# Windowed attention, MLP and linear attention in one kernel: separate orders for even and odd steps, and the second final product in another PSUM bank

## What is computed

```python
# x: (8, 128, 32, 32) float32; C=128, windows of 8x8 = 64 tokens, 8 heads of 16
win = x in windows                                  # (B*16, 64, 128)
q, k, v = split(layernorm(win) @ in_w.T + in_b)     # per head
o = softmax(q @ k.T / 4) @ v
win = win + o @ out_w.T + out_b
y = win back in rows, channels last
y = y + silu(layernorm(y) @ fc1_w.T + fc1_b) @ fc2_w.T + fc2_b     # hidden 256
# second layer, linear attention over the N=1024 tokens of an image, E=64
q, k, v = wq @ y + bq, wk @ y + bk, wv @ y + bv
out = wo @ ((q.T @ k) / N @ v.T).T + bo + y
```

## Time and profile before

| | us |
|---|---|
| median of 3 runs | 371.51 (369.45 to 372.06) |
| the profiled execution | 368.75 |
| its span, first to last instruction | 367.0 |
| outside the span | 1.75 |
| PE, DVE, ACT, POOL busy in the span | 325.3, 278.4, 243.9, 165.0 |
| mean granted TensorE clock | 0.956 of full |

### The profile page before, as it was taken

The page is one execution under the profiler, slowest core; times in us unless marked ns, Lnnn a source line. Parts: engine busy times, 40 slices in busy tenths (PEclk is TensorE's granted clock), DMA queues, the critical chain, the costliest instruction groups (busy, mean ns, idle before and its releaser), DMA issues. The chain is left out here.

```text
span 367.0 us, 9985 instructions
## 1 busy us (share of the span) xinstructions
PE 325.3 (89%) x3424; PEld 275.4 (75%) x3424; DVE 278.4 (76%) x850; ACT 243.9 (66%) x449; POOL 165.0 (45%) x177
## 2 busy tenths in 40 slices
PE   6958798989899899989898999989898999977875
PEld 6847686869787887869686887869686977856563
DVE  5565588968699887978799687978799878694652
ACT  5447476866869586757869386757869496853360
POOL 5504264645527262636437162636437352622420
PEclk9999699989999999989999899989999999998995
DMA  5230203030322123130403123130403122210011
GB/s 132 65 94 17 65 23 96 18 103 0 82 92 60 55 57 114 29 86 4 139 29 76 39 56 115 27 87 4 139 29 73 41 67 79 50 38 2 0 60 57
DMA packets 31859, 21.99 MB, mean 60 GB/s; under 512 B 22432, under 2 KB 23776, under 8 KB 31840
## 3 DMA queue, kind: packets, MB, share of 16 engines
q1 hardware_dynamic: 31744, 21.62, 21.7%
q10 hardware_dynamic: 96, 0.13, 0.2%
HBM read 4.95 MB, written 4.19 MB: 25 GB/s over the span
## 5 line engine op out<-in xcount | busy, mean ns | idle before, releaser
L1123 ACT ACTIVATE probs<-p_scoreT 128x512 f32<-128x512 f32 x64 | 38.1, 595 | 57.2 <-PE p_scoreT L751 55.2
L519 POOL TENSOR_SCALAR rstd<-mv 128x4 f32<-128x4 f32 (+1 forms) x33 | 7.5, 227 | 129.0 <-DVE mv L1307 128.7
L1366 DVE TENSOR_REDUCE row_max<-p_x 128x8 f32<-128x512 f32 x64 | 42.5, 684 | 10.9 <-PE p_x L723 10.9
L766 PE MATMUL p_attn<-vd,probs 128*64 128x34 f32 x1024 | 47.2, 246 | 0.0
L537 POOL TENSOR_TENSOR hid_l<-hid,hid_h 128x512 fp32r<-128x512 f32 x30 | 37.8, 1275 | 16.9 <-ACT hid_h L1158 8.4
L766 PEld LDWEIGHTS p_attn<-vd,probs 128*64 128x64 f32 x1024 | 37.7, 140 | 9.4 <-issue 5.5
L747 PE MATMUL p_scoreT<-qd_h,kd_h 128*128 128x256 f32 x128 | 39.6, 309 | 0.1
L529 POOL TENSOR_SCALAR kd_l<-k_l,head_a 128x512 fp32r<-128x512 f32 x15 | 23.9, 1595 | 33.7 <-issue 33.7
L521 POOL TENSOR_TENSOR rstd<-rstd,minus_half 128x4 f32<-128x4 f32 (+1 forms) x33 | 37.0, 1122 | 2.8
L747 PE MATMUL p_scoreT<-qd_l,kd_h 128*128 128x256 f32 x128 | 36.6, 286 | 0.0
L747 PE MATMUL p_scoreT<-qd_h,kd_l 128*128 128x256 f32 x128 | 36.4, 285 | 0.0
(11 more groups left out here) (239 smaller groups left out, 920.0 us busy)
## 6 DMA issues: line engine op xcount, KB each, us to landing
qd_l<-q_l SPq DMA_DIRECT2D x64, 64.0 KB, 2.0
vd<-v_tok SPq DMA_DIRECT2D x64, 64.0 KB, 2.2
qd_h<-q_h SPq DMA_DIRECT2D x62, 64.0 KB, 2.0
out<-out_sb SPq DMA_DIRECT2D x15, 256.0 KB, 2.2
x_in<-in_x SPq DMA_DIRECT2D x14, 256.0 KB, 2.9
x_first<-in_x SPq DMA_DIRECT2D x2, 256.0 KB, 3.0
fc_rows<-in_L_conv_fc_w SPq DMA_DIRECT2D x2, 128.0 KB, 2.8
out<-out_sb SPq DMA_DIRECT2D x2, 128.0 KB, 2.1
```

The source lines that it names most:

```text
L766: last = pe.matmul(p_attn[64 * win:64 * win + 64, 2 * VB * j:2 * VB * (j + 1)], probs[:, p % 2, win, j, :], vd[:, h.par, 2 * p + win, :, : ...
L1123: act.activation(probs[:, p % 2], p_scoreT[:].rearrange("row (win j q) -> row win j q", win=2, j=QUADS), ACT.Exp, scale=SCORE_SCALE).then_ ...
L1366: dve.tensor_reduce(row_max[:, p].rearrange("row (j a) -> row j a", a=2), score(p).rearrange("row j (a k) -> row j a k", a=2), AXIS_X, ALU.max
```

## The change

Each engine's `step` becomes four functions: `first_step`, `second_step`, `even_step` and `odd_step`, each with an order of its own; `prologue` and `epilogue` are rewritten. In the loop, PE calls in these orders (T0 to T3 are `b_scoreT`, A0 to A3 `b_attn`):

- before, every step: score, c_transpose, fc2, project, T0, a_back, yT, kv, a_transpose, T1, A0, (d_kvT), k, q, T2, (d_bT), A1, c_back, T3, (d_mT), A2, v, (final 0), fc1_0, (final 1), fc1_1, A3
- after, even: score, c_transpose, T0, project, T1, a_back, yT, a_transpose, A0, fc2, T2, k, q, T3, c_back, A1, kv, A2, fc1_0, v, fc1_1, A3
- after, odd: score, c_transpose, T0, fc2, project, T1, kv, yT, a_back, A0, d_kvT, T2, a_transpose, d_bT, q, k, T3, A1, c_back, d_mT, v, A2, final 0, fc1_0, fc1_1, A3, final 1

`final 1` is written to `p_scoreT` and needs `b_exp(3)` done, not the copy of `final 0`. In the loop ACT widens p = 1 and 2, DVE p = 0 and 3. In the first step, `load_silu_table` calls Exp, so the table isn't changed; `b_score` waits for `q_low` there and not for `v_kept`; the first `v` goes to `p_scoreT`. The matmuls that fold biases write `p_c[1]`, and `load_x(3)` and `load_late` are issued in SP's prologue. All instructions of the loop stay, 1 CAST of DVE per step becoming an ACTIVATE of ACT.

```diff
+        def v_bank(h):
+            return p_a[0] if h.follows(1) else p_scoreT
...
@@ SP
             def step_odd(loop, more, d):
+                if more and d:
+                    load_x(loop.half(3))
                 if more:
-                    load_x(loop.half(3))
                     spread_q(loop.half(2))
...
@@ POOL
+            def odd_step(loop):
+                rstd2_of(c)
+                y2_low_part(tail)
+                rstd1_of(next_a)
+                residual(a)
+                k_low_block(a)
+                hidden_low(c, 1)
+                hidden_low(c, 0)
...
@@ PE
-            def d_final(loop, c, half):
+            def d_final(loop, c, half, dst):
...
-                elif half == 1:
+                elif dst is p_scoreT:
+                    pe.wait_ge(probs_ready[PAIRS - 1], loop.half(1).n())
+                else:
                     pe.wait_ge(fin_kept[0], loop.image(c))
...
@@ PE b_scoreT, p == 0
+                    if h.c == 0 and h.follows(2):
+                        pe.wait_ge(fin_kept[1], h.loop.image(-1))
...
@@ ACT
+            def even_step(loop, more):
+                c_o(c)
+                load_exp_table(b)
+                b_exp(b, 0)
+                b_widen(b, 1)
+                a_xn_high(a)
+                b_exp(b, 1)
+                b_widen(b, 2)
+                a_xn_full(a)
+                b_exp(b, 2)
...
+                load_silu_table(b)
+                c_silu(c, 0)
+                a_v(a)
+                c_silu(c, 1)
+                c_y2(tail)
...
+            def odd_step(loop):
+                load_exp_table(b)
+                c_o(c)
+                b_exp(b, 0)
+                b_widen(b, 1)
...
+                d_out(loop, -1, 0, p_d)
+                c_silu(c, 0)
+                c_silu(c, 1)
+                d_out(loop, -1, 1, p_scoreT)
```

More of the change, by code:

```diff
@@ L595, in step_odd @@
             def step_odd(loop, more, d):
-                step(loop, loop.half(1), more, more, True, d)
+                if d:
+                    odd_step(loop)
+                else:
+                    second_step(loop)
             def epilogue(loop):
@@ new lines, in even_step @@
+            def even_step(loop, more):
+                b, a, next_a, c, tail = loop.half(0), loop.half(1), loop.half(2), loop.half(-1), loop.half(-2)
+                b_score(b, True)
+                c_transpose(c)
+                b_scoreT(b, 0)
+                c_project(c)
+                b_scoreT(b, 1)
+                scores_read(b)
+                a_back(a)
+                c_yT(c)
+                if more:
+                    a_transpose(next_a)
+                b_attn(b, 0)
+                c_fc2(tail)
+                b_scoreT(b, 2)
+                a_k(a)
+                a_q(a)
+                b_scoreT(b, 3)
+                c_back(c)
+                b_attn(b, 1)
+                c_kv(tail)
+                b_attn(b, 2)
+                c_fc1(c, 0)
+                a_v(a)
+                c_fc1(c, 1)
+                b_attn(b, 3)
@@ new lines, in odd_step @@
+            def odd_step(loop):
+                b, a, next_a, c, tail = loop.half(1), loop.half(2), loop.half(3), loop.half(0), loop.half(-1)
+                b_score(b, True)
+                c_transpose(c)
+                b_scoreT(b, 0)
+                c_fc2(tail)
+                c_project(c)
+                b_scoreT(b, 1)
+                c_kv(tail)
+                c_yT(c)
+                scores_read(b)
+                a_back(a)
+                b_attn(b, 0)
+                d_kvT(loop, -1)
+                b_scoreT(b, 2)
+                a_transpose(next_a)
+                d_bT(loop, -1)
+                a_q(a)
+                a_k(a)
+                b_scoreT(b, 3)
+                b_attn(b, 1)
+                c_back(c)
+                d_mT(loop, -1)
+                a_v(a)
+                b_attn(b, 2)
+                d_final(loop, -1, 0, p_d)
+                c_fc1(c, 0)
+                c_fc1(c, 1)
+                b_attn(b, 3)
+                d_final(loop, -1, 1, p_scoreT)
+                pe.wait_ge(fin_kept[0], loop.image(-1))
@@ L1489, in prologue, with first_step @@
                 a_xn(other)
[L1491 to L1498 removed]
+            def first_step(loop):
+                b, a, next_a, c, tail = loop.half(0), loop.half(1), loop.half(2), loop.half(-1), loop.half(-2)
@@ new lines, in even_step @@
+            def even_step(loop, more):
+                b, a, next_a, c, tail = loop.half(0), loop.half(1), loop.half(2), loop.half(-1), loop.half(-2)
+                b_max(b, 0)
+                b_widen(b, 0)
+                c_o(c)
+                b_max(b, 1)
+                b_max(b, 2)
+                b_max(b, 3)
+                c_y1(c)
+                c_stats(c)
+                b_widen(b, 3)
+                c_aggregate(c)
+                a_xn(a)
+                if more:
+                    a_stats(next_a)
+                b_norm(b, 0)
+                c_norm(c)
+                a_k(a)
+                c_y2(tail)
+                if more:
```

498 lines of the change are left out of this document (282 added, 216 removed).

## The result

| | before | after |
|---|---|---|
| median, same chip | 370.48 us (368.75 to 372.06, 4 runs) | 349.86 us (349.11 to 350.44, 4 runs) |
| profiled execution, its span | 368.75, 367.0 | 349.11, 347.3 |
| mean granted clock | 0.956 | 0.979 |

A forecast was written before the change was run, and what follows sets the result against it. PE, busy 89%, was taken as the bound. Loop 14, first two steps 6.3 and epilogue 3.5 sum to 23.8 us off the profiled 368.75, giving 345.0; with 2.76 for the median, 347.5 us forecast, range 339 to 358.

The forecast's parts named there:

- hid_l waits, loop: Loop: moving c_fc2 removes PE's waits for POOL's hid_l, 0.5 us per even and 1.6 per odd step, refills included.
- Second final product: Loop: its own bank and last place remove PE's waits of 0.30 and 0.40 for ACT's copies, 0.9 us with refills.
- Low clock in the loop: Odd loop steps: the 0.50 clock following the 1.52 wait goes with that wait, saving 1.1 us per pair.
- Even step, +0.8 net: Even loop step: new waits of 0.1 for max_wide, 0.6 for o_l, 0.6 for exp, sum 1.3, against 0.5 removed.
- Odd step, -2.0 net at full clock: Odd loop step: 1.6 and 0.9 removed, 0.5 added (0.2 for o_l before project, 0.3 at c_transpose).
- The loop: Six pairs: 4.1 us removed, 1.3 + 0.5 added, net 2.3 per pair; 14 taken, bounds 4 to 20.
- The lock (rule weighed, first rival): DVE's widening blocked by POOL's hid_l: 0.1 us per step in the sum; rival, blocked through both: 355.5 us, chance 0.10.
- First two steps with the prologue: Start: removed waits and low clock sum to 7.3 us, less 1.0 new waits: net 6.3, between 3 and 8.
- Epilogue: End: hid_l and yn_tok waits and low clock, 1.4 + 1.2 + 1.7, less 0.8 new waits: 3.5 us, between 0 and 6.
- ACT late: Rival, loop: ACT comes into the even step late, so a pair gains only 0.7 us; 357.5 us, chance 0.08.
- clock falls in even steps: Rival, even steps: the new waits bring the low clock in half of seven steps, 6 us; 353.5 us, chance 0.12.
- slower: Rival: widening blocked through both hid_l, PE idles over 2 us each step start, clock falls each time; 377.5 us, chance 0.03.

The follow-up runs named there:

- the kernel with two parts alone: Kernel before plus two order edits in loop and last even step: fc2 behind the first products (PE), first maximum and its widening first (VectorE); 370.53 us, ratio 1.012.

## Why the prediction was right

Forecast 347.5 us, measured 349.86, 0.7% over it. Part of that closeness is luck: the sum was 23.8 off the profiled execution, 345.0, where 349.11 was measured, 19.6 off; and 2.76 was added for the median, which this time lay only 0.75 above its profiled execution. (345.0 and 2.76 are 347.8; the recorded 347.5 is a slip of 0.3.)

To check the waits, compare starts and not idle times. The idle time of a row is counted from the modelled end of the matmul before, so a delay is longer than the idle time shown, and a short one is inside the busy time. In the odd step before, the four transposes began at 118.04 and `c_fc2` at 120.22:

```profile
118.04 0.66 PE L782 MATMUL p_c<-ident,o_tok 128*128 128x128 f32 x4
120.22 0.47 PE L620 MATMUL p_c<-hid_h,wh 128*128 128x512 f32 x1 [1.52 <-POOL hid_l L537]
```

That is 2.18, where the next group comes after 0.41 without a wait (186.95 to 187.36 above): 1.77 lost for 1.52 of idle time. By the prediction's own steps:

- **hid_l waits, loop (2.1 per pair).** Right: 1.77 and 0.60 by starts, gone, and back 13 times when fc2 went back. The "refills" are real, and a little larger than 0.15.
- **Second final product (0.9 per pair).** Right. By starts 0.47 and 0.47 went. The end of the odd step has no wait; without the bank it waits 2.04.
- **Low clock in the loop (1.1 per pair).** Right: the four odd steps had 6.2 us of it in all, 1.0 per pair. It is 1.00 in all steps after, and also in the kernel with two parts alone, in which the wait of 1.52 was gone too.
- **Even step, +0.8 net.** Measured +0.65 (17.60 to 18.25), and the steps of the working came true. By starts the new waits are 0.1 for `max_wide`, 0.63 for `o_l` and 0.47 for `probs` (forecast 0.1, 0.6, 0.6), with a tenth or two of smaller delays 1.4 where the sum had 1.3; 0.60 went, where it had 0.5. The 0.15 that is missing to +0.8 is groups that follow each other more cheaply.
- **Odd step, -2.0 net at full clock, the step of the working that was off.** Measured -1.25 (22.21 to 20.96). The waits come out as forecast in sum: by starts 2.7 went (forecast 2.5) and 0.75 came (forecast 0.5), together -2.0. They stand elsewhere, though: 0.5 ahead of the `max_wide` products, for which the prediction had nothing, 0.24 at the project, and none at `c_transpose`, where it had 0.3. The latter has a reason in the rows: `kd_l` on VectorE, 0.86 in the earlier trace rows, took 0.48 after, as GpSimd's instruction that it overlapped before was moved. What the sum had at nothing is the other 0.7: groups of matmuls that wait for nothing but have other neighbours than before, and start the next group later. Three such places make up 0.55 (last section). Over six odd steps it is 4 us, more than the whole shortfall of the loop.
- **The loop: 10.6 instead of 14**, within the bounds of 4 to 20. Odd steps of 20.9 lie just outside the 20 to 20.8 that the prediction gave as a sign of being right.
- **The lock (rule weighed, first rival).** The 0.1 per step was right in the even step (CAST 0.52) and too low in the odd one (0.81). In the even step VectorE got its turn between GpSimd's two `hid_l` (169.55 to 170.07), so the rival, in which it waits for both, fell. The Trainium skill, page "SBUF — State Buffer", section "SBUF: two separate sides", says that of a VectorE instruction in a fast mode and a GpSimd instruction the second is blocked for the whole instruction of the first; the trace agrees, with the ends 0.28 or 0.29 apart in five cases. The expected length of 0.7 to 1.0 came true in odd steps only.
- **First two steps with the prologue, 6.3; measured 7.0.** The waits of the earlier trace rows are gone, but single parts are not shown: the load of the table was one of the named causes, and putting it back costs nothing. The prologue's 1.7 isn't shown to be the change's: a kernel with the start of before unchanged had its first `b_score` at 17.34, and those with the start of after at 16.8 to 17.5. And this stretch takes 32.4 to 35.9 in twelve profiles with the same code there up to one table load and the split `hid_l`; the low clock falls at different places in them; before it took 37.9 and 39.2. The size is uncertain by more than 1 us.
- **Epilogue, 3.5; measured 2.4.** Within its bounds of 0 to 6, but by the old order put back only 0.7 of the 2.4 is the new order's.
- **ACT late, clock falls in even steps, slower.** None came: ScalarE stands idle for 0.38 before the even step's `o_h`, which it begins at 169.48, and with the idle times of 0.46, 0.34 and 0.21 that PE has in the loop the clock stayed at 1.00.

## What to carry to other kernels

When a wait is removed by moving work out from under it, the moved work leaves its own cover behind: here fc2's old place hid the waits for `o_l` and `probs`, and its next place the way to `a_k`. Look for work that can be cut at an accumulation boundary and put half into each gap; that gave about 2% more on top of a large reorder. Undo parts of a bundle before crediting them: two of its parts without the others gave nothing, and undoing the place of fc2 or the new bank cost 20 and 14 us, together more than the whole gave. And when you forecast a new order, leave room for what the groups cost each other: here it was 0.7 us of a step of 21 that no wait shows.

## What the runs showed of the hardware

**A waiting VectorE instruction gets its turn as soon as GpSimd's instruction ends**, even if GpSimd has the next one queued. Then GpSimd's next takes longer: 1.46 for `y_l` right behind the CAST, and a mean of 1387 ns for `hid_l` after, which takes 1.28 undisturbed. The page after, the costliest groups:

```profile
L542 POOL TENSOR_TENSOR hid_l<-hid,hid_h 128x512 fp32r<-128x512 f32 x30 | 41.3, 1387 | 18.1 <-ACT hid_h L1248 17.5
```

**What follows a group of matmuls changes its cost.** PE before, in order of time, where products of the scores follow four transposes:

```profile
131.13 0.65 PE L801 MATMUL p_c<-ident,yn_tok 128*128 128x128 f32 x4
131.54 0.36 PE L747 MATMUL p_scoreT<-qd_h,kd_h 128*128 128x256 f32 x1
```

and after, where `d_mT` follows the same transposes:

```profile
161.19 0.66 PE L831 MATMUL p_c<-ident,yn_tok 128*128 128x128 f32 x4
161.78 0.48 PE L884 MATMUL p_x<-bT,wq_rows 64*128 64x128 f32 x2
```

0.41 before the next group starts in one order, 0.59 in the other, with no wait shown and the clock at 1.00. In the same two odd steps `v` (eight matmuls) takes 0.91 to the next start ahead of a final product and 1.09 ahead of `b_attn`, and `a_transpose` 0.35 ahead of `b_scoreT` and 0.54 ahead of `d_kvT`. In all three the dearer neighbour is a product of small matmuls (34 to 128 columns). PE's busy time of an odd step rose from 19.98 to 20.62 with the same 224 instructions; 0.7 of the step is such cost by starts, 4 us in the loop. In the even step (17.23 to 17.58) the starts show 0.15 less of it, and the rise there is short delays counted as busy. No order was tried to win the 4 us back, and why some neighbours cost more is open.
